# Graph-attention edge stage: scaling weights read from a PSUM bank, right logits in one bank instead of two

## The reference, cut to what matters

```python
feat_all = jnp.einsum('ni,rhid->rnhd', inputs, conv_weights)
feat_src_e = feat_all[edge_type, edge_src]
el = jnp.sum(feat_src_e * attn_l[edge_type], axis=-1)
er = jnp.sum(feat_dst_e * attn_r[edge_type], axis=-1)
e = leaky_relu(el + er, negative_slope=0.2)
m = segment_max(e, edge_dst)
ex = jnp.exp(e - m[edge_dst])
denom = segment_sum(ex, edge_dst)
alpha = ex / denom[edge_dst]
h = segment_sum(alpha[..., None] * feat_src_e, edge_dst) + h_bias
```

## Time and profile before

| | us |
|---|---|
| median of 3 runs | 2340.95 |
| lowest and highest of the runs | 2340.59, 2343.41 |
| the profiled execution | 2339.81 |
| its span, first to last instruction | 2337.9 |
| mean granted TensorE clock over the span | 0.854 of 2.4 GHz |

### The profile page before, as it was taken

How to read it: one execution, slowest core, us unless ns; L and a number is a source line. 1 busy time by engine, 2 the same in 40 slices (tenths; PEclk the granted TensorE clock), 3 DMA queues, 4 the chain that set the end, 5 groups by cost and what they waited for, 6 DMA issues and landing times. The chain is left out here.

```text
span 2337.9 us, 38560 instructions
## 1 busy us (share of the span) xinstructions
PE 1894.4 (81%) x9138; PEld 1599.3 (68%) x9139; DVE 1140.2 (49%) x3045; ACT 850.0 (36%) x2164; POOL 1242.5 (53%) x1138
## 2 busy tenths in 40 slices
PE   6999866887787778778877877877453999999998
PEld 5788755666666666666666666656342888888887
DVE  5233135666666665666666666667761111111211
ACT  1222453453453454444444444431182222222221
POOL 4000277777777777777777777775073222222222
PEclk9999857887888887887888878878655999999999
DMA  5443333333333343343343333332335566666664
GB/s 186 173 179 135 140 106 105 102 105 104 101 103 105 102 106 105 100 106 102 103 106 106 101 107 102 103 102 70 95 132 193 167 190 193 197 199 194 189 189 124
DMA packets 120339, 305.69 MB, mean 131 GB/s; under 512 B 26711, under 2 KB 72535, under 8 KB 106484
## 3 DMA queue, kind: packets, MB, share of 16 engines
q0 software_dynamic: 61344, 150.28, 25.0%
q1 hardware_dynamic: 58836, 153.86, 19.1%
HBM read 246.07 MB, written 60.08 MB: 131 GB/s over the span
## 5 line engine op out<-in xcount | busy, mean ns | idle before, releaser
L642 POOL DMA_INDIRECT gath<-feats,idxT x996 | 1040.6, 1045 | 529.6 <-issue 289.2
L932 PE MATMUL psP<-gath,hot 128*128 128x260 f32 x1992 | 598.3, 453 | 31.8 <-DVE gath L753 31.5
L932 PEld LDWEIGHTS psP<-gath,hot 128*128 128x128 f32 x1992 | 425.9, 225 | 111.6 <-DVE gath L753 23.2
L919 PE MATMUL psE<-er,hotT 128*128 x1992 | 316.8, 309 | 119.7 <-issue 115.7
L919 PEld LDWEIGHTS psE<-er,hotT 128*128 128x128 f32 x1992 | 303.2, 233 | 160.1 <-issue 159.5
L858 ACT COPY hotT<-psOT 128x512 f32<-128x512 f32 x249 | 145.0, 582 | 585.9 <-PE psOT L905 585.4
L1377 POOL DMA_INDIRECT out<-yrow,node x74 | 115.1, 1555 | 436.1 <-DVE yrow L1485 421.9
L848 ACT ACTIVATE hot<-cst,ndlT 128x128 f32<-128x128 f32 x996 | 317.6, 393 | 6.3 <-PEq L288 6.3
L753 DVE TENSOR_TENSOR gath<-gath 128x1024 f32<-128x1024 f32 x249 | 302.4, 1224 | 9.9 <-ACT gath L877 2.3
L762 DVE TENSOR_TENSOR acc<-acc,psP 128x260 f32 x498 | 210.3, 422 | 188.2 <-PE psP L932 79.0
L1441 ACT ACTIVATE hT<-psH,w1buf 128x256 f32<-128x256 f32 x296 | 123.9, 470 | 387.8 <-PE psH L1404 387.8
(11 more groups left out here) (207 smaller groups left out, 1169.8 us busy)
## 6 DMA issues: line engine op xcount, KB each, us to landing
w1buf<-in_experts SPq DMA_DIRECT2D x37, 1030.0 KB, 8.1
w2buf<-in_experts SPq DMA_DIRECT2D x37, 1024.0 KB, 5.2
feats<-frow SPq DMA_DIRECT2D x30, 1040.0 KB, 3.9
gath<-feats,idxT POOLq DMA_INDIRECT x996
xrow<-slots_x SPq DMA_DIRECT2D x37, 258.0 KB, 6.4
meta<-in_edges SPq DMA_DIRECT2D x464, 12.0 KB
b_all<-in_b SPq DMA_DIRECT2D x37, 128.0 KB, 6.2
xs<-xb SPq DMA_DIRECT2D x5, 768.0 KB, 9.8
```

The source lines that it names most:

```text
L642: pool.indirect_dma_start(gath[:, r, u], None, feats, bass.IndirectOffsetOnAxis(ap=idxT[:, r, u:u + 1], axis=0)).then_inc(gath_in[r], 16)
L919: ins = pe.matmul(psE[:, u * W // 512, u * W % 512:u * W % 512 + W], hotT[:, j % 2, k * P:(k + 1) * P], tables[k // BLK], start=True, stop ...
L932: ins = pe.matmul(psP[:, bank(g, b, r), 0:FW], hot[:, r, u], gath[:, r, u], start=u % BLK == 0, stop=u % BLK == BLK - 1)
```

## The change

- `psE` shrinks to one bank; the bank that this frees is the new `psA`.
- ACT writes the exponentials twice (new L879 and L880): into `psA`, at 128 columns for each of the three ring positions, and as before into the logit columns of `gath`, which `total` still reads for the denominators. `exp_ready` follows the second.
- `scale` reads its weights from `psA` instead of `gath`. The features are read and written in `gath` as before.
- `pick_right` does one half a call. Half 0 of group g+1 stands after `chain_maxima(g)`, half 1 where both stood. `picked` counts halves. After half 0, DVE waits for its own `picked`.
- PE waits for half 0 to be picked before it writes quad 4 of the same group into the one bank.
- `BANKS` stays 4.

```diff
-        psE = psum("psE", [P, 2, 512])
+        psE = psum("psE", [P, 512])
         psS = psum("psS", [P, 512])
+        psA = psum("psA", [P, 512])
...
-                def pick_right(g, r):
+                def pick_right(g, r, b):
 
                     half = GU // 2
-                    dve.wait_ge(er_done, quads_before(g) + quads(g))
+                    us = slice(b * half, (b + 1) * half)
+                    dve.wait_ge(er_done, quads_before(g) + min(quads(g), (b + 1) * SLOTS_Q // 2))
...
+                    dve.tensor_reduce(er_e[:, us], all4, AX.X, ALU.add).then_inc(picked, 1)
+                    if b == 0:
+                        dve.wait_ge(picked, g * 2 + 1)
...
-                    alpha = gath[:, r, j * QUAD:(j + 1) * QUAD, D:FW]
+                    alpha = psA[:, r * P + j * QUAD * HEADS:r * P + (j + 1) * QUAD * HEADS].rearrange("p (u h) -> p u h", h=HEADS)
...
                     chain_maxima(g)
+                    if there(g + 1):
+                        pick_right(g + 1, rn, 0)
                     add(a, 4, ra, sums4)
...
                     if there(g + 1):
-                        pick_right(g + 1, rn)
+                        pick_right(g + 1, rn, 1)
...
+                            act.activation(psA[:, r * P:(r + 1) * P], psS[:, S_DT:S_DT + P], ACT.Exp)
                             act.activation(gath[:, r, :, D:FW], psS[:, S_DT:S_DT + P].rearrange("p (u h) -> p u h", h=HEADS),
...
+                    if j == SLOTS_Q // 2:
+                        pe.wait_ge(picked, g * 2 + 1)
```

More of the change, by code:

```diff
@@ L662, in meta_columns @@
                     index_columns(dve, sb, psS, r).then_inc(idx_ready, 1)
-                def pick_right(g, r):
+                def pick_right(g, r, b):
                     half = GU // 2
-                    dve.wait_ge(er_done, quads_before(g) + quads(g))
+                    us = slice(b * half, (b + 1) * half)
+                    dve.wait_ge(er_done, quads_before(g) + min(quads(g), (b + 1) * SLOTS_Q // 2))
                     all4 = er_all[:].rearrange("p (u h r) -> p u h r", u=half, r=RELS)
[L669 to L676, removed]
+                    step(dve.tensor_tensor(all4, psE[:].rearrange("p (u h r) -> p u h r", r=RELS, h=HEADS),
+                                           typeT[:, r, us].unsqueeze(2).to_broadcast([P, half, HEADS, RELS]), ALU.mult))
+                    dve.tensor_reduce(er_e[:, us], all4, AX.X, ALU.add).then_inc(picked, 1)
+                    if b == 0:
+                        dve.wait_ge(picked, g * 2 + 1)
                 def logits(g, r, n):
-                    dve.wait_ge(picked, g + 1)
+                    dve.wait_ge(picked, g * 2 + 2)
                     dve.wait_ge(gath_in[r], landed(g, r, n))
@@ L773, in _ @@
                 step(dve.memset(lv[:, 5, GU:GU + 1], 0.0))
-                pick_right(0, 0)
+                for b in range(2):
+                    pick_right(0, 0, b)
                 logits(0, 0, 0)
-                STEPS = 30
+                STEPS = 29
                 prologue = []
@@ L916, in right_logits @@
                     pe.wait_ge(hotT_copied, quads_before(g) + j + 1)
+                    if j == SLOTS_Q // 2:
+                        pe.wait_ge(picked, g * 2 + 1)
                     for k in range(QUAD):
                         u = j * QUAD + k
-                        ins = pe.matmul(psE[:, u * W // 512, u * W % 512:u * W % 512 + W], hotT[:, j % 2, k * P:(k + 1) * P],
+                        ins = pe.matmul(psE[:, u * W % 512:u * W % 512 + W], hotT[:, j % 2, k * P:(k + 1) * P],
                                         tables[k // BLK], start=True, stop=True)
@@ L941, in _ @@
                     turn(1, 1, j)
-                pe.wait_ge(picked, 1)
+                pe.wait_ge(picked, 2)
                 right_logits(1, 0)
@@ L980, in period @@
                     if there(g + 2):
-                        pe.wait_ge(picked, g + 2)
+                        pe.wait_ge(picked, g * 2 + 4)
                     right_logits(g + 2, 0)
```

## The result

The changed kernel takes 2254.89 us (median of 4 runs, 2251.93 to 2256.29), against 2340.77 us for the kernel before in the same comparison (4 runs). The ratio is 0.9631, with a 95% interval of 0.9614 to 0.9648: 3.7% faster. The forecast was 2258 us, with a range of 2250 to 2286.

What follows compares the result with a forecast made beforehand. The prediction took POOL's gather stream, held up by scalings with two SBUF inputs, as the bound. 2339.8 - 84.0 + 0.1 x 3 + 0.3 = 2256.4 us profiled, so 2258 us (-3.5%), range 2250 to 2286.

Steps and rivals of the forecast that it cites:

- The bound and the mechanism: Edge stage: POOL's gather stream sets the 43.25 us period; scalings with two SBUF inputs hold gathers up.
- The stall term: Gather hold-ups over 29 periods: 29 x (43.25 - 40.27) = 86.4 us, less 2.4 us that stay, so 84.0 us go.
- The 2.4 us of excess beside other instructions: Gathers with no scaling beside them: their 2.4 us above 0.953 us each was to stay.
- Duration of the scaling: `scale` on DVE: stays at 1224 ns with weights from PSUM, cost taken as 0.
- Second exponential: ACT: 0.15 to 0.3 us more, covered in a full period; +0.3 us once in the last group.
- Half of the pick moved, PE's new wait: DVE does 1.41 us of pick earlier, given back later but for +0.1 us; PE's wait before quad 4 costs 0 to 0.2.
- the price of +0.1 us: DVE's wait for its own `picked` after the early half pick: +0.1 us a period, bounds 0 and 0.3.
- What is late next: After the change POOL, at 40.35 us a period, stays the bound by 0.4 us over the DVE/PE loop.
- the loop's length: Loop of DVE and PE without the gather wait: 39.86 us, plus 0.1 makes 39.96 us a period.
- The rival of a loop that takes over: The DVE/PE loop becomes the bound, from 0.4 us more a period: 2280 us, range 2262 to 2288, chance 0.24.
- The tail: End of the edge stage: 0.1 x 3 us for the last loop-bound periods, plus 0.3 us for the exponential.
- The sum: Profiled execution: 2339.8 - 84.0 + 0.1 x 3 + 0.3 = 2256.4 us, 1.1 us under the median of runs.

Runs made afterwards that it cites:

- sbuf_weights: The changed kernel with the second exponential and the scaling weights in an SBUF tile of their own instead of the PSUM bank: 2370.17 us, ratio 1.0124.
- half_psum: The changed kernel with even quads scaled by weights from PSUM and odd quads by weights from SBUF: 2316.25 us, ratio 0.9895.
- turns_only: The changed kernel with weights read from `gath` again and no second exponential; right-logit halves still alternate in one bank, half the pick moved: 2370.28 us.
- weights_only: The kernel before with scaling weights in a PSUM bank taken from the sums (three banks left), both halves picked late: 2288.49 us, ratio 0.9768.
- before_filled: The kernel before with one spare DVE reduction of 512 elements (0.7 us) ahead of the pick: 2368.36 us, ratio 1.0111.

## Why the prediction was right, point by point

**The bound and the mechanism.** Right. The hold-up came from the second SBUF input (`sbuf_weights`, `half_psum`), and without it the gathers run at their floor: period 40.32 us, predicted 40.27 + 0.08. The stall term was 84.0 us; the 29 periods gave 85.04. The 2.4 us of excess beside other instructions were to stay: 2.0 us are left. One reading was miscounted: between 300 and 1640 us not 148 but 231 gathers start inside a scaling. 146 of them take more than 1.0 us, and these hold the 88 us. The other 85 start in the last 0.17 us of a scaling and aren't held up. By the same count 150 gathers start inside an `add`, not 83, all at 0.95 or 0.96 us. The sum doesn't use these counts, but the 85 are the first sign of what `turns_only` showed. The Trainium skill's rule that a two-input DVE instruction contends with a GpSimd read ("SBUF — State Buffer", Who interferes with whom) agrees with the three runs that tell it apart (`sbuf_weights`, `half_psum`, `weights_only`). The Trainium skill's remark in the same section that `tensor_tensor` left DMAs issued from GpSimd alone doesn't fit these indirect DMAs: the gathers beside a `tensor_tensor` took 1.78 and 1.82 us instead of 0.95.

**Duration of the scaling.** Right: 1220 against 1224 ns. The estimated 65 ns that the Trainium skill's page "VectorE: DVE Perf Modes" (The TRN2 errata) would add for a PSUM operand didn't come.

**Second exponential.** Right at no cost. ACT, then the DVE scaling that waits for it:

```profile
787.79 0.27 ACT L879 ACTIVATE psA<-psS 128x128 f32<-128x128 f32 x1
787.99 0.27 ACT L880 ACTIVATE gath<-psS 128x128 f32<-128x128 f32 x1
```

```profile
789.15 1.22 DVE L752 TENSOR_TENSOR gath<-gath,psA 128x1024 f32<-128x1024 f32 x1
```

It adds 0.20 us and ends at 788.26, 0.89 us ahead of the scaling.

**Half of the pick moved, PE's new wait.** Right for the kernel as a whole. DVE's half pick and the add behind it, then PE's right logits of quad 4 and total of quad 6:

```profile
779.61 0.69 DVE L671 TENSOR_TENSOR er_all<-psE,typeT 128x512 f32<-128x512 f32 x1 [0.17 <-DVE lv L723]
780.33 0.69 DVE L673 TENSOR_REDUCE er_e<-er_all 128x64 f32<-128x512 f32 x1
781.17 0.43 DVE L761 TENSOR_TENSOR acc<-acc,psP 128x260 f32 x1
```

```profile
781.40 1.91 PE L924 MATMUL psE<-er,hotT 128*128 x8 [0.66 <-ACT hotT L860]
783.64 3.83 PE L937 MATMUL psP<-gath,hot 128*128 128x260 f32 x8 [0.34 <-DVE gath L752]
```

The add comes 1.56 us after the pick starts (predicted 1.41 + 0.1). PE goes on 0.38 us after the pick's end (0.3), but what it waited for there is ACT's copy `hotT`; from 400 to 1400 us PE's waits for the pick come to 0.5 us in all. The total takes 3.83 us, at the lower level. But the price of +0.1 us holds only together with the weights in PSUM. Alone, the move costs 29 us, because the distance from one scaling to the next decides which gathers are held up. I had priced the move by what it displaces and not by what it changes in phase. That this did no harm to the forecast wasn't foreseen: it cancelled because the same change ends all hold-ups. By this path the change is +29 us for the move and -115 us for the weights.

**What is late next.** Half right. POOL is still the bound, but not by 0.4 us: 18 of 29 logit sums wait for no gather, and 0.69 us a period costs 13 us. Logit sums are 40.3 us apart only on the mean; single ones are 37.3 to 43.6 us apart. The step that was mis-sized is the loop's length, which I took as one number, 39.96 us. As a mean that is about right (39.7 us without the first period), but the loops are spread from 37.3 to 43.6 us, with TensorE's clock and with DVE's branch. The rival of a loop that takes over was closer than its 0.24 made it look. Three banks for sums would have brought it about.

**The tail.** Predicted +0.6 us; measured +0.4 us in the last two groups.

**The sum.** The prediction had 2256.4 us for the profiled execution, and it took 2256.29. That they agree to 0.1 us is luck: the periods gave 1.0 us more than the 84.0, and terms that weren't in the sum (+2.33 us before the first logit sum, -1.1 us in the later stages) took it back.

## What to carry to other kernels

If a DMA issued by GpSimd bounds a kernel, look in the two timelines for DMA instructions that start inside a DVE instruction with two SBUF inputs; putting one small operand in PSUM frees them. A bank of PSUM for it has its own price, so look for the bank whose loss the schedule can hide, and measure that loss in a kernel that is no longer held up by the old bound. While such hold-ups remain, the distance between two DVE instructions matters: adding 0.7 us of work to an engine with idle time cost 25 us, and adding 1.4 us to `turns_only` won 20. And a mean loop below the bound isn't room: look at the spread of its lengths, and at what recurs every few periods.

## What was not expected of the hardware

- A held-up gather ends about 0.83 us after the scaling does, so the next starts 1.13 us after it: each hold-up sets the stream's phase for those that follow. Which scaling is hit is therefore largely regular: for quad 3, 1 of 30 groups in the kernel before and 30 of 30 in `before_filled`.
- A gather whose start comes up to about 0.1 us before the scaling's end, or 0.14 us ahead of its start, is not held up (877.20 and 875.94 above).
- DVE's branch at the end of the loop body is followed by 2.8 to 3.7 us in which DVE does nothing, 27 us over its eight times in the changed kernel.
- Without that branch, the same list of work in the changed kernel takes 37.3 us at a mean granted clock of 0.91 and up to 42.8 us at 0.72. Why the clock is high in some periods and low in others wasn't tried.
